# Loads of x, the order of the x1 and chunk sends, and the T differences moved between engines in a two-layer LoRA kernel

## What is computed

```python
# layer 0: gated feed-forward with a LoRA of rank 16 per batch, then a binarized linear layer
gate = x @ W_gate.T + lora(x, A_gate[id0], B_gate[id0]) * 0.5      # 1376 wide
up   = x @ W_up.T   + lora(x, A_up[id0],   B_up[id0])   * 0.5
act  = silu(gate) * up
c0   = act @ W_down.T + lora(act, A_down[id0], B_down[id0]) * 0.5   # 512 wide
x1   = x + c0 @ sign(weight).T + bias0
# layer 1: a low-rank condition, then a linear layer with eight weighted LoRAs
c1   = (x1 @ B[id1].T) @ A[id1].T
out  = x1 + c1 @ W.T + bias + sum_n 2 * w_n * (c1 @ lora_A[n].T) @ lora_B[n].T
```

## Time and profile before

| | us |
|---|---|
| median of 3 runs | 891.04 (883.05 to 893.37) |
| the profiled execution | 893.9 |
| its span | 891.8 |
| TensorE busy in it | 857.4 |
| VectorE, ScalarE, GpSimd busy | 644.5, 289.9, 99.5 |

### The profile page before, as it was taken

How to read it: one execution, slowest core, us unless ns; L and a number is a source line. 1 busy time by engine, 2 the same in 40 slices (tenths; PEclk the granted TensorE clock), 3 DMA queues, 4 the chain that set the end, 5 groups by cost and what they waited for, 6 DMA issues and landing times.

```text
span 891.8 us, 22271 instructions
## 1 busy us (share of the span) xinstructions
PE 857.4 (96%) x7384; PEld 699.8 (78%) x7384; DVE 644.5 (72%) x1354; ACT 289.9 (33%) x535; POOL 99.5 (11%) x130
## 2 busy tenths in 40 slices
PE   8998899998999999999999999999999999999897
PEld 5886688886788788888888888878788788878785
DVE  5695676866768586877868686877868586877764
ACT  4861432322333232333333232322333232323310
POOL 0256000100000000000000000000000000000001
PEclk9999999999999999999999999999999999999999
DMA  9977877877877797888879787888779697888753
GB/s 337 415 257 251 311 222 227 253 243 251 263 249 214 219 298 246 273 278 270 272 240 260 233 258 244 286 264 271 234 255 254 218 293 246 279 266 272 232 142 102
DMA packets 171356, 227.31 MB, mean 255 GB/s; under 512 B 59200, under 2 KB 128832, under 8 KB 163648
## 3 DMA queue, kind: packets, MB, share of 16 engines
q1 hardware_dynamic: 112800, 114.47, 43.6%
q10 hardware_dynamic: 56096, 103.37, 33.7%
q0 software_dynamic: 2432, 9.11, 2.7%
HBM read 178.69 MB, written 16.97 MB: 219 GB/s over the span
## 4 chain that ended last, share of the span: by engine, by line
PE 64%; DMA 13%; SPq 9%; DVE 7%; issue 3%; ACTq 1%; ACT 1%; POOL 0%; DVEq 0%
PE gu_ps L1238 33%; PE y_ps L1359 19%; DMA x_landed<-x_in 6%; SPq L370 3%; DMA x_in<-in_x 2%; PE out_ps L1381 2%; PE gu_ps L1468 2%; PE out_ps L1432 2%; SPq L396 2%; DMA landed<-act_all 1%; SPq L462 1%; SPq L457 1%; DMA xT_raw<-in_xT 1%; PE out_ps L1368 1%; DVE act_all L923 1%
## 5 line engine op out<-in xcount | busy, mean ns | idle before, releaser
L1359 PE MATMUL y_ps<-down_sb,actT_sb 128*128 128x512 f32 x1023 | 247.9, 395 | 0.0
L1359 PEld LDWEIGHTS y_ps<-down_sb,actT_sb 128*128 128x128 f32 x1023 | 189.7, 188 | 59.4 <-issue 21.4
L571 POOL TENSOR_TENSOR b_two<-b_raw,const_sb 128x128 f32<-128x128 f32 x62 | 23.8, 404 | 684.8 <-DMA b_raw<-in_b1tab 684.8
L640 ACT CAST actT_sb<-landed 128x512 fp32r<-128x512 f32 (+1 forms) x96 | 51.8, 582 | 148.1 <-issue 114.8
L1238 PE MATMUL gu_ps<-wg_sb,xT_sb 128*128 128x432 f32 x384 | 84.1, 369 | 2.8 <-DVE act_all L923 2.8
L1238 PE MATMUL gu_ps<-wu_sb,xT_sb 128*128 128x432 f32 x384 | 81.7, 361 | 0.0
L1238 PEld LDWEIGHTS gu_ps<-wg_sb,xT_sb 128*128 128x128 f32 x384 | 72.9, 193 | 8.1 <-DVE xT_sb L905 3.7
L1238 PEld LDWEIGHTS gu_ps<-wu_sb,xT_sb 128*128 128x128 f32 x384 | 71.0, 188 | 4.0
L1238 PE MATMUL gu_ps<-slot,s_sb 128*128 128x512 f32 x270 | 69.0, 391 | 0.0
L927 DVE STREAM_TRANSPOSE act_all<-act_all 128x512 f32<-128x512 f32 (+1 forms) x96 | 64.1, 667 | 3.3
L640 ACT COPY ad_two<-a_raw 128x352 f32<-128x352 f32 x64 | 28.0, 484 | 118.2 <-PE out_ps L1381 114.5
(11 more groups left out here) (188 smaller groups left out, 1295.0 us busy)
## 6 DMA issues: line engine op xcount, KB each, us to landing
slot<-t_table ACTq DMA_DIRECT2D x59, 1024.0 KB, 8.0
vslot_raw<-vt_table ACTq DMA_DIRECT2D x60, 432.0 KB, 4.5
a_raw<-in_atab SPq DMA_DIRECT2D x128, 152.0 KB, 8.0
rows_sb<-in_btab SPq DMA_DIRECT2D x128, 118.0 KB, 3.6
landed<-act_all SPq DMA_DIRECT2D x192, 64.0 KB, 3.1
xT_raw<-in_xT SPq DMA_DIRECT2D x32, 256.0 KB, 3.8
x_in<-in_x SPq DMA_DIRECT2D x31, 256.0 KB, 9.9
out_x<-out_sb SPq DMA_DIRECT2D x31, 256.0 KB, 6.1
```

The costliest lines, as they stand in the source:

```text
L571: nc.gpsimd.tensor_tensor(b1_two[:, n].rearrange("p k e r -> p e k r"), rows, ones, ALU.mult).then_inc(L["b1_moved"], 1)
L640: return nc.scalar.copy(o, i)
L1359: last = nc.tensor.matmul(to[:], actT_sb[:, ACTT_SLOT[c] + n, a, :], down_sb[:, blk, b, :], start=begin and (c, n) == (0, 0) and (a, b) == ...
```

## The change

- SP loads x of step g at the end of step g, once x1 of the step before has landed, instead of in step g+1 behind the A rows.
- xT of the step after next is loaded by ScalarE behind `copy_lhs` instead of by SP behind ad_moved.
- In an odd step SP sends quarters 0 and 1 of chunk 1 only, and x1's quarters ahead of the c rows. ScalarE sends quarters 2 and 3 of chunk 1 in the next even step behind `copy_q1`, then its half of x1, both ahead of `high_s(4)`.
- ScalarE does Silu ahead of `high_s(1)` and `high_s(2)`; VectorE does `low_s(1)`, `low_s(2)` behind the gates and `low_side_t(1)`, `low_side_t(2)` behind `turn_x1`.
- The T and side differences are made by VectorE in step 0 (before `low_t(1)`, and behind the gates). GpSimd stores T1, T2, side 1 and 3, T3, T4, side 2 and 4 in this order; vt_out becomes two semaphores.
- In the last step `down` of chunk 0 of step 30 goes behind the rows, and `down_rows` opens the sum.

```diff
+
+        def load_xT(engine, g, parity):
+            engine.dma_start(xT_raw[parity][:], xT[bass.ds(g * P, P), :].rearrange("p (k t) -> p k t", k=KC)
+                             ).then_inc(xT_in(parity), 16)
...
                 sp.wait_ge(L["ad_moved"], PAIRS * (g + 1))
-                if after_next is not None:
-                    load_xT(after_next, parity)
...
                 if prev is not None:
                     if isinstance(prev, int) and prev == 0:
                         sp.wait_ge(S["last_out"], 2 * 32)
-                    load_x(prev)
+                        load_x(prev)
...
                     if parity == 1:
-                        send_act(sp, g, 1)
+                        send_act(sp, g, 1, range(0, 2))
                     send_act(sp, g, 2)
-                    if prev is not None:
+                    if prev is not None and parity == 1:
+                        send_x1(sp, prev, range(2, 4))
+                        load_c(sp, post)
+                    elif prev is not None:
                         load_c(sp, post)
                         send_x1(sp, prev, range(2, 4))
                     load_b(next_cond)
+                    if prev is not None:
+                        sp.wait_ge(L["x1T_in"], SENT * (prev + 1))
+                        load_x(g)
...
-            def difference(o, a, b):
-                nc.gpsimd.tensor_tensor(o[:], a[:], b[:], ALU.subtract).then_inc(S["t_raw"], 1)
-
-            pool.wait_ge(S["raw1_in"], 32)
-            pool.wait_ge(S["block_lo"], 4)
-            difference(t1_raw, t3_raw, t1_raw)
-            pool.wait_ge(S["raw2_in"], 32)
-            pool.wait_ge(S["t_raw"], t_count(1))
-            difference(t3_raw, t2_raw, t3_raw)
-            pool.wait_ge(S["t_raw"], t_count(3))
-            difference(t2_raw, t2_raw, t1_raw)
-            pool.wait_ge(S["t_raw"], t_count(2))
-            difference(t4_raw, t4_raw, t2_raw)
...
+            def side_store(n, signal):
+                pool.wait_ge(S["vt_raw"], 4)
+                pool.dma_start(vt_table[n - 1], vt_raw[n][:].rearrange("p k w -> p (k w)")).then_inc(signal, 16)
+
             t_store(1, S["first_out"])
-
-            def side_difference(o, a, b):
-                nc.gpsimd.tensor_tensor(vt_raw[o][:], vt_raw[a][:], vt_raw[b][:], ALU.subtract).then_inc(S["vt_raw"], 1)
-
-            pool.wait_ge(S["vraw_in"], 4 * 16)
-            side_difference(1, 3, 1)
-            pool.wait_ge(S["vt_raw"], t_count(1))
-            side_difference(3, 2, 3)
-            pool.wait_ge(S["vt_raw"], t_count(3))
-            side_difference(2, 2, 1)
-            pool.wait_ge(S["vt_raw"], t_count(2))
-            side_difference(4, 4, 2)
-            pool.wait_ge(S["vt_raw"], t_count(4))
-            for n in range(1, 5):
-                pool.dma_start(vt_table[n - 1], vt_raw[n][:].rearrange("p k w -> p (k w)")).then_inc(S["vt_out"], 16)
             t_store(2, S["first_out"])
+            side_store(1, S["vt13_out"])
+            side_store(3, S["vt13_out"])
             t_store(3, S["last_out"])
             t_store(4, S["last_out"])
+            side_store(2, S["vt24_out"])
+            side_store(4, S["vt24_out"])
...
-            def step(g, j, parity, prev, pp, nxt):
+            def step(g, j, parity, prev, pp, nxt, after_next):
                 if parity == 0 and seven(j):
                     copy_p1(j)
                     copy_q1(j)
+                    send_act(act, prev, 1, range(2, 4))
+                    send_x1(act, pp, range(0, 2))
                     high_s(4, j)
                     load_side_t(3)
-                    send_x1(act, pp, range(0, 2))
                 if isinstance(g, int) and g == 1:
-                    act.wait_ge(S["vt_out"], 4 * 16)
+                    act.wait_ge(S["vt13_out"], 2 * 16)
                 if prev is not None:
                     split_actT(prev, 0)
                 if parity == 0 and seven(j):
@@ -739,6 +723,8 @@
                     high_t(2)
                 move_ad(g)
                 copy_lhs(g)
+                if after_next is not None:
+                    load_xT(act, after_next, parity)
                 if parity == 0 and seven(j):
                     load_t(3, L["slot0_in"])
                     load_t(4, L["slot1_in"])
...
+                    if not seven(j):
+                        act.wait_ge(S["vt24_out"], 2 * 16)
...
+                for c in range(NC):
+                    silu(g, c)
                 if parity == 1 and nxt is not None:
                     high_s(1, j + 1)
                     high_s(2, j + 1)
-                for c in range(NC):
-                    silu(g, c)
-                if parity == 1 and nxt is not None:
                     high_side_t(1, j + 1)
                     high_side_t(2, j + 1)
                 send_act(act, g, 0)
...
+            def differences(raw, signal):
+                def difference(o, a, b):
+                    nc.vector.tensor_tensor(raw[o][:], raw[a][:], raw[b][:], ALU.subtract).then_inc(signal, 1)
+
+                difference(1, 3, 1)
+                dve.wait_ge(signal, t_count(1))
+                difference(3, 2, 3)
+                dve.wait_ge(signal, t_count(3))
+                difference(2, 2, 1)
+                dve.wait_ge(signal, t_count(2))
+                difference(4, 4, 2)
...
                 if first(g):
-                    dve.wait_ge(S["t_raw"], t_count(2))
+                    dve.wait_ge(S["raw1_in"], 2 * 16)
+                    dve.wait_ge(S["raw2_in"], 2 * 16)
+                    differences(t_raw, S["t_raw"])
                     low_t(1)
...
                 if nxt is not None:
                     split_xT(nxt, 1 - parity)
-                if parity == 1 and nxt is not None:
-                    low_s(1, j + 1)
-                    low_s(2, j + 1)
                 if pp is not None:
                     after(dve, L["stored"], 16 * pp)
                     add_out(pp)
...
                     gated(g, c)
                     turn_act(g, c)
                 if parity == 1 and nxt is not None:
-                    low_side_t(1, j + 1)
-                    low_side_t(2, j + 1)
+                    low_s(1, j + 1)
+                    low_s(2, j + 1)
                 if first(g):
+                    dve.wait_ge(S["vraw_in"], 4 * 16)
+                    differences(vt_raw, S["vt_raw"])
                     low_t(3)
                     low_t(4)
...
                 if prev is not None:
                     add_y(prev)
                     turn_x1(prev)
+                if parity == 1 and nxt is not None:
+                    low_side_t(1, j + 1)
+                    low_side_t(2, j + 1)
                 if last(g):
                     split_actT(g, 1)
...
-            def down_rows(n, to=y_ps):
+            def down_rows(n, to=y_ps, begin=False):
                 return nc.tensor.matmul(to[pair(n), :], lhs_sb[group(3), pair(n)], rows_sb[group(3), n, 0:H],
-                                        start=False, stop=False, skip_group_check=True)
...
                     if prev is not None:
-                        down_rows(n)
+                        down_rows(n, begin=begin)
...
                 if prev is not None:
                     after(pe, L["x1_done"], prev)
-                    down(prev, 0, begin=True).then_inc(L["y_mm"], 1)
+                    if not last(g):
+                        down(prev, 0, begin=True).then_inc(L["y_mm"], 1)
                 lora_ready(g, j, parity, prev, pp)
-                first_rows(prev, pp)
+                first_rows(prev, pp, last(g))
                 second_rows()
                 if prev is not None:
-                    for c in range(1, NC):
+                    for c in range(0 if last(g) else 1, NC):
                         down(prev, c).then_inc(L["y_mm"], 1)
```

More of the change, by code:

```diff
@@ L273, in build_adaln_ffn @@
                  "weff_hi", "weff_lo", "a1_hi", "a1_lo", "c_mm", "c_out", "wg_hi", "wg_lo", "wu_hi", "wu_lo",
-                 "wmid1_in", "wmid2_in", "wside1_in", "wside2_in", "block_hi", "block_lo", "raw1_in", "raw2_in", "vraw_in", "vt_raw", "vt_out", "t_raw", "t_hi", "t_lo", "first_out", "last_out",
+                 "wmid1_in", "wmid2_in", "wside1_in", "wside2_in", "block_hi", "block_lo", "raw1_in", "raw2_in", "vraw_in", "vt_raw", "vt13_out", "vt24_out", "t_raw", "t_hi", "t_lo", "first_out", "last_out",
                  "silu_ready", "pad_set", "bias0_in", "bias0_added")
@@ L478, in _ @@
             sp.dma_start(v22_raw[:], wside[:, half(3)]).then_inc(S["wside2_in"], 16)
-            def load_xT(g, parity):
-                sp.dma_start(xT_raw[parity][:], xT[bass.ds(g * P, P), :].rearrange("p (k t) -> p k t", k=KC)
-                             ).then_inc(xT_in(parity), 16)
             def load_x(g):
@@ L535, in _ @@
             rows_stored(sp)
-            load_xT(1, 1)
+            load_xT(sp, 1, 1)
             sp.dma_start(t3_raw[:], wmid[:, KC:KC + HALF]).then_inc(S["raw1_in"], 16)
@@ L888, in _ @@
```

(22 more changed lines are left out.)

## The result

The changed kernel takes 865.46 us (median of 4 runs, 863.23 to 865.62); the kernel before took 891.52 us beside it (4 runs, 883.05 to 893.37). The ratio is 0.971, 95% interval 0.965 to 0.977: faster by 2.3 to 3.5%. The profiled execution took 865.62 us, its span 863.8 against 891.8 of before. Ratios leave out runs that lie more than 1.5% above the fastest of their kernel.

The account below looks back on a forecast made before the run. TensorE is busy 857.4 of 891.8 us, so only its 34.4 us idle could be won. Loop 15.6, start 8.0 and last step 0 sum to 23.6 us; 870.3, less 2.9 to the median, gives 867.4 us (range 861 to 879).

Parts of the forecast that it names:

- The start: Step 0 and step 1: differences on VectorE and reordered stores remove waits and slow products, 8.0 us won (bounds 0 and 9.3).
- the wait for the rows: Step 1: TensorE reaches the rows at 92.0, left operands stand at 92.7, so it waits 0.7 us.
- The loop's idle time: Loop waits of TensorE for x1 (14.3 us) and the gates (3.3 us), 17.6 us, all taken as won before q5's price.
- 2.0 for q5: Even steps: block q5 waits for side parts moved behind x1, slack 0.2 us in a mean pair; 2.0 us lost.
- the transposed x: Loop, issued by ScalarE: no change in a usual pair, bounds 1 us either way; 3.3 us won in one late pair.
- The add of the bias: Even steps on GpSimd (1.29 us): starts beside the side parts; VectorE goes first, so only the second side part is late.
- The clock: Start: twelve products behind a gap took 4.04 us against 2.51; 1.5 us counted back without the gap.
- The last step: down of chunk 0 behind the rows: rows at most 0.8 us earlier, products end 1.4 later; taken as 0.
- x early, the order and the sends together: Loop: x loaded a step sooner, VectorE parts reordered, x1 sent 3.6 us earlier; removes the 14.3 us wait for x1.
- Rival 1: Even steps: the side part becomes the wait, q5 stands 0.7 us in each of 15 pairs; 876 us, chance 0.10.
- Rival 4: Loop: the transposed x lands 4.4 us later than the mean, q5 stands 4.2 us a pair; 930 us, chance 0.03.
- Rivals 2 and 3: Start keeps its waits, only renamed: 875 us, chance 0.08; x1 still lands last in the loop: 874.5 us, chance 0.05.

Follow-up runs that it names:

- undo_start: Kernel after with T and side differences on GpSimd again, with the old stores and waits: 872.1 us.
- bias_first: Kernel after with GpSimd adding the bias to x1 ahead of moving the layer 1 rows: 865.16 us.
- undo_last: Kernel after with down of chunk 0 ahead of the last rows again: 865.6 us.
- x_order: Kernel after with x loaded in the step that adds to it and the old order on VectorE and ScalarE: 864.95 us.
- undo_sends: Kernel after with chunk 1 whole on SP, x1 on ScalarE behind s4's high part and the side load, on SP behind the c rows: 878.89 us.
- x_order_xT: Kernel after with x late, the old order on VectorE and ScalarE, and the transposed x sent by SP: 879.16 us.
- undo_xT: Kernel after with the transposed x sent by SP again, behind ad_moved: 929.71 us median, from 898.34 to 944.89.
- xT_order: Kernel after with the transposed x sent by SP and the old order on VectorE and ScalarE, x still loaded early: 943.74 us.
- xT_behind: Kernel after with the transposed x issued behind the two side loads on ScalarE's queue in odd steps: 902.6 us.
- undo_x: Kernel after with x loaded in the step that adds to it again: 916.06 us, ratio 1.024 to the kernel before.

## Why the prediction was right, and where it was wrong

The forecast of 867.4 us was 1.9 too high; the steps behind it held less well than the sum. Between the two profiled executions 28.0 us of span were won where the sum has 23.6. The forecast also took off 2.9 us because the profile of before lay that far above its median; the profile of after lies 0.2 above its own. The two errors have opposite signs, so that the time came out as close as 1.9 us is in part luck. By stages, from TensorE's timelines: up to the first gate products of step 2 (116.77 against 124.37) 7.6 us, where 8.0 were forecast; from there to the small products of the last step (830.26 against 858.73) 20.9, where 15.6 were; behind them 0.5 lost, where 0 was.

**The start**: 8.0 us forecast. The rows of step 1 come 9.7 us earlier by the timelines (their waits included), less 1.7 of new waits in step 2 and 0.4 more in that stretch: 7.6. undo_start gives 8.1 by span. VectorE's parts beside GpSimd's are short again, as argued: 1.05 us for the side part that took 3.26, 0.69 for the xT part that took 2.49. Of the terms, the wait for the rows was 0.9 (0.7 forecast, for the left operands; it was the B rows that came last) and T1's load cost 1.4 where I had 0.6.

**The loop's idle time**: 17.6 us less 2.0 for q5 forecast. The 17.6 went whole. The 2.0 never came: the slack of q5 is larger than the 0.2 us I worked with. In the mean pair VectorE waits (30.4 - 4.7) / 14 = 1.8 us for the transposed x, not 2.75, because it goes ahead of ScalarE's loads and reaches VectorE after 3.4 us instead of 4.3 (mean of 14 and of 13 pairs). I had bounded this at 1 us either way and taken none; it was worth 0.9 us in each pair. In the pair that was read, the first of the two side parts, begun at 401.34, is done near 402.3, and q5 begins at 403.24: 0.9 us of slack where the prediction had 0.63, behind a wait of 2.18 us for the transposed x. TensorE's line, and VectorE's wait over the whole span:

```profile
403.24 1.33 PE L1241 MATMUL gu_ps<-vslot,s_sb 128*128 128x432 f32 x6
```

```profile
DVE s_raw L968 <- DMA xT_raw<-in_xT: 30.4, 15, 4.7
```

against 42.9 in 14. The add of the bias does not meet the side parts at all (GpSimd is held by move_b1 until its B rows have landed), a step I had not read; bias_first shows that the meeting would have gone as I argued.

**The clock**: 1.5 us counted, 4.7 measured in busy time. I priced only the products behind the first gap. The small products of the loop, which stood behind x1's waits, take 34.8 us instead of 36.6 (L1384), and those of L1371 and L1392 0.6 less together, a term that I left out.

**The last step**: 0 forecast, 0.5 us longer by the timelines, nothing by undo_last. The rows' wait was 1.7 us; that x1's last quarters would then be waited for, 1.3 us, I did not see. Against these 3.0 us stand 2.4 us of waits for the landed chunks that went (1.5 and 0.9 in the kernel before).

**Who earned it.** Here the prediction's account fails. It gave 14.3 us to x early, the order and the sends together and 3.3 to the transposed x, and it costed x early at nothing because "SP's queue then holds only the next step's loads". The runs give: x early and the order together 0 (x_order), the sends 7.2 us by span and 13 by the medians (undo_sends), the transposed x by ScalarE 10.2 and 14 with x late and the old order (x_order_xT against x_order), and 33 to 79 with x early and the new order (undo_xT). By the medians the parts come to more than the 26 us of the whole, so they are not shares of it; no run adds the sends or the transposed x alone to the kernel before. The sentence on SP was the mis-step. It holds only because the transposed x had left that queue; with it there, x early makes it 0.7 to 1.0 us late, and the kernel becomes as slow as before or slower (898 to 955 us in undo_xT and xT_order). I read the move of the transposed x as a change of issuer with bounds of 1 us, while it decides whether it goes ahead of 2.9 MB of T loads. The page of before had the evidence: its wait of 7.2 us is the pair in which SP issued 1.79 us behind ScalarE's first side load (202.48 and 200.69), and I had even named SP's lateness as its cause.

**The rivals.** Rival 1 (the side part becomes the wait) did not come in the kernel after, but its mechanism is real: a late x sets it off, 2.6 us a pair. Rival 4 (the transposed x lands late) is real too, with a price of the right order: by its rule 3.7 us of lateness cost 52 us, and xT_behind costs 37; xT_order costs 65 in its fastest run. It did not come because the transposed x goes out 0.4 us ahead of the T loads, which the diff shows. Rivals 2 and 3 are refuted by the lists of waits.

## What to carry to other kernels

A change of several moves is not a sum of them: here one move (x1 ahead of the side parts) is harmless only with a second (x early, by undo_x and x_order), and that one only with a third (the transposed x on ScalarE's queue, by undo_xT and x_order_xT). Before costing a moved load at nothing, list what the queue that issues it, and the engine that waits for it, do next, and price that lateness. And issue what is wanted first ahead of the large loads: one place later on the same queue cost 37 us here. Across queues the traces point the same way, so compare issue times between queues, in each pair of steps, not only the median landing.

## What the runs showed of the hardware

**A small DMA behind large ones.** The transposed x is 256 KB; the T loads are 2 x 432 KB and 2 x 1024 KB. From its issue to VectorE's first use of it, by how far it was issued behind ScalarE's first side load: 2.8 to 4.1 us if 0.4 ahead of it (kernel after, 14 pairs); 3.9 to 4.4 at 0.02 to 0.15 behind (x_order_xT, 12 pairs; the kernel before, 8); 4.1 to 4.6 at 0.4 to 0.6 (the kernel before, 5 pairs; x_order_xT, 1); 4.8 to 8.5 at 0.7 (undo_xT, 13 pairs); 7.5 to 9.1 at 0.9 to 1.4 (xT_order, 12 pairs). Of the two pairs of xT_order that are left, one at 0.76 took 4.8 and one at 2.76 took 8.8; the one of undo_xT, at 3.09, took 9.0. The first T load follows the first side load by 0.84 us in undo_xT, x_order_xT and xT_order; beyond that point the transposed x comes 7.1 to 9.5 us after its issue, about as late as the T loads themselves (8.8 us in xT_order).

In undo_xT and xT_order x (256 KB) also lies ahead of it on SP's queue, so those pairs do not tell the two causes apart. In x_order_xT and the kernel before it does not, and their two late pairs (1.44 and 1.79 us behind) took 9.5 and 7.1 us: two pairs are all that speaks for ScalarE's loads alone. The Trainium skill (DMA: Bandwidth & Descriptors, Queues, rings and completion order) says that each DMA engine goes round between the queues that have work, a packet at a time. By that alone a 256 KB load on SP's queue would share the engines with ScalarE's loads and not wait for all of them. In these pairs it comes about as late as they do; whether it stands behind them or gets a small share beside them, no run here shows. The same page of the Trainium skill (Issuing engines are not separate DMA queues) says that another issuer saves only issue time. xT_behind agrees in this: on ScalarE's queue, but behind the side loads, the gain of the move is gone.

**The clock behind waits.** Behind a wait of 2.1 us (undo_x) the granted clock of the next 5 us was 0.66, behind one of 4.55 us (xT_order) 0.50, which is the lower level throughout. In undo_x the products behind the waits took 13.8 us longer, beside 36.9 us of waits.
